# Turning the second pair's value product on VectorE in 32 by 32 squares instead of on TensorE, in an RWKV block with an FFN

## The reference

```python
z = norm(x)
h = layer_norm(z, ln1_g, ln1_b); hh = shift(h)
k, v, r = ((h * m + hh * (1 - m)) @ W.T for m, W in ((tm_mk, Wk), (tm_mv, Wv), (tm_mr, Wr)))
z1 = z + (sigmoid(r) * wkv(k, v)) @ Wo.T
h = layer_norm(z1, ln2_g, ln2_b); hh = shift(h)
kv = silu((h * cm_mk + hh * (1 - cm_mk)) @ Wkey.T) @ Wval.T          # 512 -> 2048 -> 512
x2 = x + z1 + sigmoid((h * cm_mr + hh * (1 - cm_mr)) @ Wcr.T) * kv
out = x2 + (silu(n @ Wg.T) * (n @ Wu.T)) @ Wdown.T,  n = norm(x2)    # 512 -> 2 * 2048 -> 512
```

## Time and profile before

| | |
|---|---|
| time, median of 3 runs | 1042.97 us (1042.65 to 1043.96) |
| the profiled execution | 1042.62 us, its span 1040.8 us |
| granted TensorE clock | 1.0 of full speed |
| PE busy | 1030.8 us, 99% |
| DVE, ACT, POOL busy | 746.1, 538.9, 664.5 us |
| DMA | 197.09 MB, 189 GB/s |

### The profile page before, as it was taken

How to read it: one execution, slowest core, us unless ns; L and a number is a source line. 1 busy time by engine, 2 the same in 40 slices (tenths; PEclk the granted TensorE clock), 3 DMA queues, 4 the chain that set the end, 5 groups by cost and what they waited for, 6 DMA issues and landing times.

```text
span 1040.8 us, 13820 instructions
## 1 busy us (share of the span) xinstructions
PE 1030.8 (99%) x4607; PEld 850.6 (82%) x4607; DVE 746.1 (72%) x1240; ACT 538.9 (52%) x902; POOL 664.5 (64%) x541
## 2 busy tenths in 40 slices
PE   8999999999999999999999999999999999999998
PEld 6777888888888888878888888888888888888887
DVE  7899866786576687586568577788689466666655
ACT  7866888857444445355354534333435344444442
POOL 7796673726676875777747565678683456665652
PEclk9999999999999999999999999999999999999999
DMA  9100325367867787989924565964945455445432
GB/s 349 59 21 0 60 66 118 102 204 266 329 219 292 266 277 245 353 310 313 284 99 164 196 227 172 239 236 142 298 164 196 152 169 177 149 153 162 160 103 81
DMA packets 98854, 197.09 MB, mean 189 GB/s; under 512 B 40160, under 2 KB 53344, under 8 KB 93920
## 3 DMA queue, kind: packets, MB, share of 16 engines
q1 hardware_dynamic: 74880, 146.84, 41.3%
q0 software_dynamic: 15168, 48.24, 15.1%
q10 hardware_dynamic: 8736, 1.14, 1.2%
HBM read 117.00 MB, written 74.99 MB: 184 GB/s over the span
## 4 chain that ended last, share of the span: by engine, by line
PE 86%; DVE 5%; POOL 5%; ACT 2%; issue 2%; DMA 0%; SPq 0%; ACTq 0%; DVEq 0%; POOLq 0%
PE bank L941 14%; PE bank L943 14%; PE bank L942 14%; PE bank L930 10%; PE bank L931 10%; PE bank L932 10%; POOL operand L2605 3%; PE bank L1121 2%; PE bank L1122 2%; PE bank L1123 2%; PE bank L1143 2%; PE bank L1141 2%; PE bank L1142 2%; POOL weights L2593 1%; PE bank L1005 1%
## 5 line engine op out<-in xcount | busy, mean ns | idle before, releaser
L941 PE MATMUL bank<-combo,left 128*128 128x512 f32 x672 | 262.2, 390 | 0.4 <-ACT made L1571 0.2
L943 PE MATMUL bank<-combo,left 128*128 128x512 f32 x672 | 261.5, 389 | 0.0
L942 PE MATMUL bank<-combo,left 128*128 128x512 f32 x672 | 261.5, 389 | 0.0
L2640 POOL TENSOR_TENSOR left<-quart,left 128x512 fp32r<-128x512 f32 x96 | 115.9, 1230 | 74.5 <-ACT left L1447 43.4
L941 PEld LDWEIGHTS bank<-combo,left 128*128 128x128 f32 x672 | 126.1, 188 | 28.6 <-ACT bank L1685 0.8
L943 PEld LDWEIGHTS bank<-combo,left 128*128 128x128 f32 x672 | 126.1, 188 | 26.4
L942 PEld LDWEIGHTS bank<-combo,left 128*128 128x128 f32 x672 | 126.1, 188 | 25.9
L2679 POOL TENSOR_TENSOR inner<-made,inner 128x512 fp32r<-128x512 f32 x64 | 86.1, 1368 | 61.6 <-ACT inner L1562 61.5
L2117 DVE TENSOR_TENSOR resid<-bank,resid 128x512 f32<-128x512 f32 x120 | 80.9, 686 | 51.5 <-PE bank L932 50.6
L2605 POOL TENSOR_TENSOR operand<-made,operand 128x512 fp32r<-128x512 f32 x64 | 83.2, 1353 | 34.2 <-ACT operand L1324 34.2
L930 PE MATMUL bank<-right,inner 128*128 128x512 f32 x256 | 99.6, 389 | 0.0
(11 more groups left out here) (232 smaller groups left out, 2364.9 us busy)
## 6 DMA issues: line engine op xcount, KB each, us to landing
kept_left<-left SPq DMA_DIRECT2D x24, 1792.0 KB, 8.6
left<-kept_left POOLq DMA_DIRECT2D x24, 1024.0 KB, 8.1
left<-kept_left POOLq DMA_DIRECT2D x24, 768.0 KB, 4.9
val_w<-kept_w SPq DMA_DIRECT2D x25, 512.0 KB, 5.7
quart<-wide SPq DMA_DIRECT2D x24, 512.0 KB, 3.8
tall_staged<-tall SPq DMA_DIRECT2D x32, 256.0 KB, 4.8
raw<-kept SPq DMA_DIRECT2D x32, 256.0 KB, 8.5
kept_w<-right SPq DMA_DIRECT2D x26, 256.0 KB, 7.1
```

The costliest lines, as they stand in the source:

```text
L941: pe.matmul(acc[:], hi, combo[:, c, k, 0, :], start=fresh and k == 0, stop=False, skip_group_check=True)
L942: pe.matmul(acc[:], hi, combo[:, c, k, 1, :], start=False, stop=False, skip_group_check=True)
L943: mm = pe.matmul(acc[:], lo, combo[:, c, k, 0, :], start=False, stop=k == 1, skip_group_check=True)
L2640: lo = pool.tensor_tensor(left[u % 2][:, 1, a[0]:a[0] + n, :], quart[:, a[0] + 1:a[0] + 1 + n, :], left[u % 2][:, 0, a[0]:a[0] + n, :].bit ...
```

## The change

Four things:

1. `turn_value` and ACT's `value_turned` are gone. In unit 17 DVE turns the squares of block 2 (before `sum_v`) and of block 3 (after the gates), from `resid[:, j]` to `raw[j % 2]`.
2. SP moves the squares back to `resid[:, j]`, eight transfers of 64 KB in each of units 17 and 18 (block 2), 19 and 20 (block 3). Semaphores `kv_moved`, which are those of the first loads, replace `kv_copied`; `load_fin` of a block's first two tiles waits for its moves, since they read the tile buffer.
3. The pieces of block 2 begin one unit later (unit 18, slot 1), and its first tiles are loaded in that same unit, behind the moves. PE's first out tiles of unit 18 wait for DVE's last value addition only.
4. The power of block 1 stands at the start of unit 12 on POOL, behind the low parts.

```diff
-FIRST_PIECE = {PAIRS: 2 * (KEYS + 1) + 1, PAIRS + 1: 2 * (KEYS + 6) + 1}
+FIRST_PIECE = {PAIRS: 2 * (KEYS + 2) + 1, PAIRS + 1: 2 * (KEYS + 6) + 1}
...
-FIN_UNIT |= {(j, s): piece_unit(j, s - 1 if s >= 2 else 0) - (s < 2) for j in FIRST_PIECE for s in range(SUBS)}
+FIN_UNIT |= {(j, s): piece_unit(j, s - 1 if s >= 2 else 0) - (j > PAIRS and s < 2) for j in FIRST_PIECE for s in range(SUBS)}
...
+            def move_value(j, sources):
+
+                sp.wait_ge(kv_turned, SUBS * (j - PAIRS + 1))
+                for a in sources:
+                    for c in range(SQUARES):
+                        source = raw[j % 2][a * SQUARE:(a + 1) * SQUARE].rearrange("q k (s t) -> q (k s) t", s=SUBS)
+                        goal = resid[:, j][c * SQUARE:(c + 1) * SQUARE].rearrange("q k (s t) -> q (k s) t", s=SUBS)
+                        sp.dma_start(goal[:, :, a * SQUARE:(a + 1) * SQUARE],
+                                     source[:, :, c * SQUARE:(c + 1) * SQUARE]).then_inc(kv_moved[j - PAIRS], 16)
...
                 else:
                     sp.wait_ge(combo_lo, 2 * SEVEN * (2 + j // 2))
+                    if j >= PAIRS:
+                        sp.wait_ge(kv_moved[j - PAIRS], 2 * LOADED + MOVED)
...
+                if KEYS < u <= KEYS + 4:
+                    half = (u - KEYS - 1) % 2 * (SQUARES // 2)
+                    move_value(PAIRS + (u - KEYS - 1) // 2, range(half, half + SQUARES // 2))
                 for j, s in FIN_UNIT:
...
                 if KEY_OUT <= n < KEY_OUT + SUBS:
-                    pe.wait_ge(kv_copied, PAIRS * SUBS)
+                    pe.wait_ge(val_added, len(VAL_GROUPS) - VAL_READ)
...
-                if u == KEYS + 1:
-                    turn_value(PAIRS)
...
-                if u == KEYS + 1:
-                    turn_value(PAIRS + 1)
...
-            def value_turned(j):
-
-                act.wait_ge(kv_turned, SUBS * (j - PAIRS + 1))
-                for s in range(SUBS):
-                    act.activation(resid[:, j, s, :], A[s][:], ACT.Copy).then_inc(kv_copied, 1)
...
-                    dve.wait_ge(kv_copied, SUBS * (j - PAIRS + 1))
+                    dve.wait_ge(kv_moved[j - PAIRS], 2 * LOADED + MOVED)
...
+            def value_turned(j):
+
+                dve.wait_ge(val_added, len(VAL_GROUPS) - VAL_READ)
+                dve.wait_ge(combo_lo, 2 * SEVEN * 3)
+                for f in range(KT):
+                    dve.transpose(raw[j % 2][:, :, f * P:(f + 1) * P],
+                                  resid[:, j, f, :].rearrange("q (k t) -> q k t", k=KT)).then_inc(kv_turned, 1)
...
                 if u > VAL_FAR:
                     value_add(u, 3)
+                if u == KEYS + 1:
+                    value_turned(PAIRS)
...
                     gate(u, 0)
                     gate(u, 1)
+                if u == KEYS + 1:
+                    value_turned(PAIRS + 1)
...
             def unit(u):
+                if u == VAL_FAR + 1:
+                    norm(2 * BLOCKS + 1)
...
-                if u == VAL_FAR:
-                    norm(2 * BLOCKS + 1)
```

More of the change, by code:

```diff
@@ L644, in build @@
         val_three = sem("val_three")
-        kv_whole, kv_turned, kv_copied = sem("kv_whole"), sem("kv_turned"), sem("kv_copied")
+        kv_whole, kv_turned, kv_moved = sem("kv_whole"), sem("kv_turned"), x_loaded[1:3]
         b12_there = w_loaded[18]
@@ L1124, in value_group @@
                 mm.then_inc(val_done, 1)
[L1126 to L1133, removed]
             def side_product(acc, q, a, c, fresh):
@@ L1712, in unit @@
                     unit_left_hi(u + 1, 0)
-                if u == KEYS + 1:
-                    value_turned(PAIRS)
                 if 0 < u < KEY_UNITS:
@@ L1763, in unit @@
                     gate_tile(u, 1, Y)
-                if u == KEYS + 1:
-                    value_turned(PAIRS + 1)
             act.dma_start(ident[:], identity).then_inc(ident_loaded, 16)
```

## The result

The changed kernel takes **1046.92 us** (median of 6 runs, 1046.17 to 1047.21), the kernel before in the same comparison 1043.01 us (6 runs): ratio 1.0042, interval 1.0031 to 1.0053. It is slower by 3.9 us between the medians (3.2 to 5.5 us by the interval) where no change was forecast, and lies above the range. The profiled execution took 1047.15 us, its span 1045.3 us, at full granted clock.

What follows compares the result with a forecast made beforehand. TensorE, busy 99% of the span, was taken as the bound. Terms: -0.5 (unit 12) -1.9 (through unit 18) +1.3 (unit 19) +0.9 (unit 22) = -0.2 us, about 1042.8 us; range 1040.3 to 1046.2.

Steps and rivals of the forecast that it cites:

- the second pair's norm: End of unit 22: block 3's first tile directly follows block 2's statistics and transposes on VectorE; costs 0.9 us, ends 0 to 1.1.
- quarters that release holes in later units: Sign of being wrong, in units after 19: SP's queue would be the bound and the forecast sum too small.
- Transposes off TensorE: Units 17 and 18: two blocks of transposes leave TensorE, taking 3.5 us off it.
- Unit 18's first product: Starts at 584.5, 1.6 us late, held until ScalarE has done SiLU on X of unit 17.
- The rest of unit 18: Through unit 18's second product and next hole: unit 19 begins 1.9 us earlier, at 597.75.
- the lower bound of 1.43: Unit 18's later hole: its chain moves at least 1.43 us earlier, 2.35 if VectorE were no bound; 1.9 was taken.
- The second eight moves and unit 19: Moves behind the left operand's write land near 600, first tile loads 603.4, seed late: unit 19 costs 1.3 us, ends 0 and 5.
- the heavy row: Earlier trace: eight moves behind a large write and two loads, landing 15.3 us behind the write's issue; heavy end 602.9.
- The power: Unit 12: power behind GpSimd's low parts ends TensorE's wait before value group 0; gain 0.5 us, near certain.
- The third rival: Second eight moves land after about 603: unit 19 costs 3.9 to 5, units 20 and 21 perhaps one; 1046.4 us, chance 0.20.

Runs made afterwards that it cites:

- run 2: Kernel before, with only block 2's norm pieces one unit later (TensorE still turns the values): 1047.03 us, ratio 1.0045.
- run 6: Changed kernel with block 3's norm also one unit later, so the two norms stand five units apart: 1050.13 us, ratio 1.0082.
- run 7: Kernel before with both blocks' norms one unit later, five units apart: 1046.95 us, ratio 1.0051.
- run 12: Kernel before with block 2's norm one unit later and one of its second eight moves instead of eight: 1043.38 us, ratio 1.0009.
- run 9: run 8 with the write of the left operand ahead of block 2's second eight norm moves on SP: 1046.15 us, ratio 1.0041.
- run 10: run 2 with the write of the left operand ahead of block 2's second eight norm moves on SP: 1045.74 us, ratio 1.0041.
- run 8: Changed kernel, block 2's first tile loads behind unit 20's quarters, the first tile's operations behind unit 19's sum V: 1045.86 us, ratio 1.0039.
- run 14: run 8 with block 2's second eight norm moves behind unit 26's quarters on SP: 1045.51 us, ratio 1.0024.
- run 3: Changed kernel with one value move per unit instead of eight, 28 of 32 squares left unmoved: 1044.19 us, ratio 1.0021.
- run 1: Kernel before with only block 1's power put behind the low parts: 1043.07 us, ratio 1.0002.
- run 13: run 2 with block 2's second eight norm moves behind unit 26's quarters on SP: 1044.84 us, ratio 1.0019.
- run 4: Changed kernel with the left operand's write behind the moves and tile loads on SP in units 17 to 20: 1054.05 us, ratio 1.0107.
- run 11: run 9 plus unit 18's weight sums in their usual place, turning behind them, and unit 19's quarters ahead of the first eight moves: 1049.29 us, ratio 1.0079.

## Why the prediction was wrong

**The failed step** is the part on the second pair's norm. "First pieces of block 2 move from the end of unit 17 to that of unit 18 ...; block 3 stays" was costed on VectorE alone, at the end of unit 22: 0.9 us. That half was right: 0.77 measured, and by its own rows the spare time is 2.4 us rather than 2.3, which makes it 0.8. Its transfers were put at nothing, without a reason. With the norms four units apart, block 2's second eight moves stand behind a tile load of block 3 and ahead of a write, two more loads and the quarters of unit 26, five places behind on SP, and these land after VectorE wants them. That cost 1.99 us here and 4.5 in the traced execution of run 2, 1.7 of it half pace. Runs 6 and 7 (five units apart) and 12 (one move) have no such hole; runs 9 and 10 have it with the write ahead of the moves, so it is the moves and not the write's place. The earlier trace rows showed a warning, 8.06 us for eight moves instead of 5.32, and a step moved by a unit moves eight DMAs. The last sentence of the prediction names this sign, quarters that release holes in later units, but the sum held nothing for it.

The other terms:

- **Transposes off TensorE**, 3.5 forecast, 3.3 measured. Right.
- **Unit 18's first product** "at 584.5", 584.92, released by ScalarE's SiLU (L1586) with 1.43 us of idle time. Right.
- **The rest of unit 18**: unit 19 was to begin 1.9 us earlier. The shift goes from +0.33 to -0.81, 1.1 us; 0.8 was mis-sized. The chain's start did move as worked out: unit 19's quarters left SP at 586.93 instead of 588.03, 1.1 us earlier, 1.4 with the 0.33 us by which this run was late before. But VectorE then stood 0.41 us for them, and its sum V came 0.82 us earlier (1.15 with the 0.33), no more. The four sums ahead of it are slow, but no slower than before. Before:

```profile
592.01 0.50 DVE L2054 TENSOR_TENSOR quart<-quart 128x256 f32<-128x256 f32 x1
592.44 1.51 DVE L2055 TENSOR_TENSOR quart<-quart 128x256 f32<-128x256 f32 x1
593.87 1.50 DVE L2057 TENSOR_TENSOR quart<-quart 128x256 f32<-128x256 f32 x1
595.41 0.84 DVE L2059 TENSOR_TENSOR quart<-quart 128x256 f32<-128x256 f32 x1
596.18 0.69 DVE L2286 TENSOR_TENSOR bank<-bank,e 128x512 f32<-128x512 f32 x1
```

  and after:

```profile
591.12 1.55 DVE L2046 TENSOR_TENSOR quart<-quart 128x256 f32<-128x256 f32 x1 [0.41 <-DMA quart<-wide]
592.60 1.51 DVE L2047 TENSOR_TENSOR quart<-quart 128x256 f32<-128x256 f32 x1
594.03 0.95 DVE L2049 TENSOR_TENSOR quart<-quart 128x256 f32<-128x256 f32 x1
595.02 0.43 DVE L2051 TENSOR_TENSOR quart<-quart 128x256 f32<-128x256 f32 x1
595.36 0.69 DVE L2286 TENSOR_TENSOR bank<-bank,e 128x512 f32<-128x512 f32 x1
```

  In both they run beside GpSimd's low parts; where GpSimd stands, such a sum takes 0.42 us (609.60 and the two behind it). So the lower bound of 1.43 was nearly what came, and 1.9, a choice between the bounds with no row for it, was too much: with the same code in this stretch, unit 19 began 1.3 to 1.5 us earlier in runs 6, 8, 9 and 14.
- **The second eight moves and unit 19**: tile loads possible at 600, issued at 599.80. The number is right, partly by luck: it was a choice between two rows, and the moves took 9.93 us to issue, longer than even the heavy row's 8.06. The tile's loads then landed later (VectorE went on at 605.23, forecast 603.4), 5.4 us behind their issue instead of 3.4. The moves are not the reason for that, since with one move (run 3) it is 5.4 us again, from 595.95 to 601.31, with VectorE waiting 2.35 us; that the four loads share the DMA engines with the writes is likely but not shown. Unit 19 cost 2.2 us instead of 1.3, inside its bounds. Run 3 shows that the moves cause it, and run 8 that another order around the tile avoids it.
- **The power**, 0.5 us, "near certain": no gain measured (run 1). A hole in front of one matmul is no gain if the next permission follows the same chain, and its fall of 0.54 here stood behind a rise of 0.93 in the unit before, where GpSimd waited 1.5 us on a transfer.

Sum of the steps measured: +0.33, -1.14 (unit 18), +2.19 (unit 19), +0.77 (unit 23), +1.99 (unit 25), and 0.3 in smaller ones, 4.4 us against -0.2. So the term that was left out is under half of the miss; unit 18 was 0.8 us off, unit 19 0.9, and what stands ahead of unit 17 another 0.8 (+0.33 in this pair of traces against the power's -0.5). The third rival's time, 1046.4 us, is near the median, but its mechanism gave unit 19 the whole of it (3.9 to 5), and unit 19 took half of that.

The Trainium skill's rule that was weighed against the change ("DMA: Bandwidth & Descriptors", Specifications: under 512 B a transfer is read, modified and written) points the right way: the windows of runs 2 and 12, which differ by seven moves in runs of 128 B and by how soon the write follows, have the DMA engines at a share of 1.01 moving 169 GB/s and at 0.93 moving 291. That they read and write such bytes twice is shown by no run. The landing of one move alone (2.4 us in the earlier trace rows) hid this; its price shows only in a queue that is full.

## What to carry to other kernels

When a step is moved by one slot, write down the order of every queue in the new slots, transfers first, as far on as the step has followers; here the costly collision lay seven units behind the edit, between a step that the change had moved and one that it had left alone. Small strided transfers cost little alone and much in front of others: look at what is queued behind them and at whether a large write is in flight. Before taking an idle hole as a gain, look whether its releaser's chain is late for the next matmul too.

## What the runs showed that was not expected

- **Issue time depends on what is in flight.** Eight moves of 64 KB in runs of 128 B take 5.3 us of SP in most places without a large write just ahead (649.12 in the earlier trace rows, 690.03 in run 13), and 5.7 to 13.4 us with a write of 1792 KB issued up to 5.4 us ahead (13.4, or 1.7 us each, in run 10). Where block 3's tile loads stood between as well, it was 9.9 to 11.9 us (runs 2 and 3 and the changed kernel), against 6.5 to 8.1 where they did not (the kernel before and runs 6 and 7).
- **The clock after a hole.** Behind idle times of 2.11 to 4.26 us TensorE's starts were 0.43 us apart, which is the lower level (1.2 GHz), for some eight matmuls, which cost 1.4 to 1.7 us more (in run 10's trace 14 and 2.9 us). In run 2 the granted clock of that stretch reads 0.50 with TensorE busy throughout:

```profile
705.70:708.70 3.00, 3.00 (x8) 2.32 (x7) 0.69 (x1) 0.60 (x1) 3.00 (x3) 0.50 0.23 66
```

  Holes of up to 1.68 us did not bring it, nor did three longer ones (2.83 us in run 4, 2.75 and 2.07 us in run 11), so the idle time alone does not decide it. A hole of 2 us may thus cost almost double; in the traced execution of run 8 that took back what the new order had saved.
- **Runs differ ahead of unit 17** with the same code there (but for the power): the shift is -1.0 to +0.6 us, and +1.8 in run 4. Part of it arises at the hole of 506.92, where the jump is 0 to 1.5 us. So single profiles were compared by jumps and not by totals.
